# Second batch's tokens ahead of most weights in the load queue; GpSimd forms T3 and T1 of the first pair, VectorE normalises the second batch's rows

## The chip, the cores and the metric

The kernel runs on one NeuronCore of one Trainium2 chip. The metric is device microseconds of one launch. Engines are named as in the profile: PE (TensorE matmuls), PEld (its weight loads), DVE (VectorE), ACT (ScalarE), POOL (GpSimd) and SP, whose queue (SPq) issues every DMA of this kernel.

## The reference

Four batches of 512 tokens by 512 features. Cut to what matters:

```python
def xattn(teacher_logits, ctx, Wq, bq, Wk, bk):           # ctx: 4 x 512 x 256
    query, key = ctx @ Wq.T + bq, ctx @ Wk.T + bk          # 4 x 512 x 128
    attention = softmax(query @ key.T, axis=-1)            # 4 x 512 x 512
    return einsum('bln,bmn->blm', teacher_logits, attention)

def ffn(x, W_up, W_gate, W_down):                          # 512 -> 2048 -> 512
    # each weight: round(w / mean|w|) clipped to -1, 0, 1, times mean|w|
    up, gate = x @ ternary(W_up).T, x @ ternary(W_gate).T
    return (silu(up) * gate) @ ternary(W_down).T

x = x + tanh(g_xattn[0]) * xattn(layernorm(x), ctx, Wq, bq, Wk, bk)
x = x + tanh(g_ffn[0]) * ffn(layernorm(x), W_up, W_gate, W_down)
```

The scale of a ternary weight is the mean of all its absolute values, so no unit of it can be rounded before all of it has been loaded and summed.

## The kernel before, in words

**Two stages.** In the first, the attention stage, PE computes for each batch b queries and keys, the energies, the transposed softmax, and then the mix of tokens with attention. DVE adds the mixed result to the token rows in `x_sb`, takes their statistics and normalises them into `xf`. In the second stage, 16 numbered units n of the feed-forward layer run over pairs of batches: (0, 1) and then (2, 3). It begins with the first `product1(0)`, lines 870 and 872.

**Products of quarters.** Matrix products are done in Winograd's form: seven products of quarter blocks in place of eight, with sums of blocks as operands. The sums of the normalised rows are called T1 to T4; B11, B21 and B22 are plain blocks. `xf_half(b, h)` is one half of the features of batch b's normalised rows. T3 is `xf_half(1,1) - xf_half(1,0)`; T1 is `xf_half(1,0) - xf_half(0,0)` and is written over `xf_half(1,0)`, so it must follow T3; T2 and T4 are made from them later. Each such block is written as a high and a low half of 16 bits (`high_t` on ACT, L1141; `low_t` on DVE, L1545), and SP transposes both by DMA for PE. The mixing of batches 0 and 1 is in the same form: `mix_product(b, j)` (PE, L786) with j in the order 1, 5, 6, 3, 7, 2, 4. Its operands are sums of the transposed tokens, made by `x_sums(b)` (POOL, L573 to L578) from `xT`, and sums of the attention, made by `p_sums_1(b)` and `p_sums_2(b)` (POOL, L582 to L589). Batches 2 and 3 are mixed plainly, by `mix(b, i)` (L763), a tile of 128 tokens at a time.

**Every engine has its order written out by hand**, and waits for the others by semaphores. The orders around the change:

- SP issues the loads one after the other. `load_ug(m, c)` (L400) is 1 MiB of the up (m = 0) or gate (m = 1) weight, `load_x(b)` (L389) 1 MiB of token rows, `load_xt(b, i)` (L397) 256 KiB of transposed tokens, `load_ctx(b)` (L386) 512 KiB of context. `load_ctx(2)` waits for PE to have read the context before it.
- POOL runs `x_sums(1)`, then four short groups of scalar arithmetic for layer norm, in this order: `rstd1_two(1,0)`, `rstd2_two(0,0)`, `rstd1_two(1,1)`, `rstd2_two(0,1)` (L558 to L568), then `p_sums_1(1)` and `p_sums_2(1)`. rstd1 is for the statistics of the token rows as loaded, rstd2 for those after the mix. `x_sums(1)` begins with a wait for all four tiles of batch 1's transposed tokens. Later POOL normalises batch 1's rows (`norm_x1`, L594, four tiles), and then in `rstd2(2, i)` and `rstd1(2, i + 2)` (L600, L601 and L548 to L551) serves batch 2, with three small instructions (L649 to L651) between that make the scales of the weights.
- ACT takes the sums of absolute values with `sum_abs(m, c)` (L1086), the exponentials with `exp_row(b, i)` (L1100), scales the rows with `norm_p` (L1105), copies transposed attention with `copy_at` (L1109), and makes the high halves, T3 and T1 among them.
- DVE adds the mix with `add_mixed(b, j)` (L1505, batches 0 and 1) or `make_x1(b, i)` (L1493, batches 2 and 3), takes the rows' maxima (`row_max`, L1471), the reciprocals of the exponential sums (`row_rsum`, L1475) and the statistics (L1482 to L1519), normalises (`norm_x1`, L1527) batches 0, 2 and 3, and makes T3 and T1 of the first pair (L1636, L1638) behind `norm_x1(2, 0)`.

"Two" in a helper's name means two tiles at once. `hold` is a wait with an empty instruction behind it, so that the engine itself stops.

Of the kernel before, what the change touches and what calls it, by code (L numbers as in the profile page):

```python
# [6 lines left out]
def gated_block_kernel(nc, x, xT, first, ctxT, wqkT, wugT, wdT, x1_dram, out):  # L7
# [19 lines left out]
    NT = ROWS // P  # L27
    NE = wdT.shape[1]
    WCOLS = NE * KD * P
    NABS = 4  # L30
# [15 lines left out]
    with stack:  # L46
# [103 lines left out]
        s_half = sem("s_half")  # L150
        s_ss, s_ts, s_mp, s_xe, s_x2p = (sem(n) for n in ("s_ss", "s_ts", "s_mp", "s_xe", "s_x2p"))
        s_dt, s_ev, s_shift = sem("s_dt"), sem("s_ev"), sem("s_shift")
# [229 lines left out]
        def _(sp):  # L382
# [39 lines left out]
            load_x(1)  # L422
            load_ug(0, 1)
            load_ug(0, 2)
            load_ctx(2)
            load_ug(0, 3)
            load_ug(1, 0)
            for i in range(NT):
                load_xt(1, i)
                if i < 3:  # L430
                    load_ug(1, i + 1)
            load_x(2)
# [87 lines left out]
        def _(pool):  # L520
# [69 lines left out]

            def norm_x1(b, i):
                hold(pool, s_r2, b * NT + i + 1)
                g = b * NT + i
                pool.tensor_scalar(xn_tile(b, i), rows(x_tile(b, i)), mv2[:, g, 0:1], r2[:, g:g + 1],  # L594
                                   ALU.subtract, ALU.mult).then_inc(s_x2p, 1)

            def rstd2(b, i):
# [37 lines left out]
            rstd1(2, 1)  # L635
            for h in range(2):
                rstd2_two(1, h)
                norm_x1(1, 2 * h)
                norm_x1(1, 2 * h + 1)
            for b in range(NS, NB - 1):  # L640
                for i in range(NT):
                    rstd2(b, i)
                    if i + 2 < NT:
# [430 lines left out]
        def _(act):  # L1074
# [86 lines left out]
            for b in range(NB):  # L1161
# [18 lines left out]
                for i in range(NT):  # L1180
# [42 lines left out]
                    if last:  # L1223
                        if i == 0:
                            act.wait_ge(s_t2, 1)
                            high_t(0, "T2", xf_half(0, 0))
                            act.wait_ge(s_x2p, NT)
                            high_t(0, "B22", xf_half(1, 1))
                            round_unit(1)
                        if i == 1:  # L1230
                            sign_unit(1)
                        if i == 2:
                            round_unit(2)
# [81 lines left out]
            def sign_down(c):  # L1315

                act.wait_ge(s_dround, c)
                act.wait_ge(d_spill, 16 * 8)
                act.wait_ge(s_x2n, NG - NT if c > 1 else 2 * NT)
                act.activation(t_d[:, c * ACOLS:(c + 1) * ACOLS], xt_flat[:, :], ACT.Sign, bias=nmagic).then_inc(s_tda, 1)  # L1320
# [10 lines left out]
            for n in range(G1 - 1):  # L1331
# [50 lines left out]
                if n == 5:  # L1382
                    act.wait_ge(s_td, 4)
                    act.wait_ge(s_x2n, NG - NT)
                    high_t(NU, "B11", xf_half(2, 0))
# [82 lines left out]
        def _(dve):  # L1468
# [102 lines left out]
            for b in range(NS):  # L1571
# [28 lines left out]
                if b == 0:  # L1600
                    rows_in(1, 3)
                    norm_x1(0, 0)
                    norm_x1(0, 1)
                else:
                    low_t(0, "B21", xf_half(0, 1))

            for b in range(NS, NB):
                last = b == NB - 1
                for i in range(NT):
# [23 lines left out]
                    if b == 2:  # L1633
                        if i == 0:
                            hold(dve, s_x2p, NT)
                            dve.tensor_tensor(t3_sb, xf_half(1, 1), xf_half(1, 0), ALU.subtract).then_inc(s_t3, 1)  # L1636
                            hold(dve, s_t3, 1)
                            dve.tensor_tensor(xf_half(1, 0), xf_half(1, 0), xf_half(0, 0), ALU.subtract)\  # L1638
                                .then_inc(s_t1, 1)
                        if i == 1:  # L1640
# [102 lines left out]
            for n in range(G1 - 1):  # L1743
# [57 lines left out]
                if n == 4:  # L1801
                    norm_x1(NB - 1, 2)
                    norm_x1(NB - 1, 3)
                    hold(dve, s_x2n, NG - NT)
                    dve.wait_ge(d_tb["T4"], d_tb_done(0, "T4"))
# [153 lines left out]
```

## Time and profile before

| | us |
|---|---|
| median of 3 runs | 412.23 (411.55 to 412.46) |
| the profiled execution, its own time | 412.31 |
| its span, first to last instruction | 410.5 |
| PE busy | 391.2 (95%) |
| DVE busy | 316.2 (77%) |
| ACT busy | 267.3 (65%) |
| POOL busy | 173.6 (42%) |

The profiled execution's own time is 1.8 us longer than its span. Times in the rows are counted from the span's start. The attention stage ends at 109.3 us, where the first `product1` starts; a change in the attention stage is worth what it moves that start, unless a later wait takes it back.

### The profile page before, as it was taken

Reading aid. Unit: us, or ns where it says so; the run is one execution under the profiler, and the core shown is the slowest. Engines: PE = TensorE matmul, PEld = TensorE weight load, DVE = VectorE, ACT = ScalarE, POOL = GpSimd, SP = SyncE. Lnnn points to the kernel's source line nnn. Section 1 sums busy time; section 2 is a strip of 40 time slices with the busy share of each in tenths; the row PEclk is TensorE's granted clock in tenths of the full one; section 3 lists DMA queues with packets and bytes.
Section 4 is the critical chain, followed back from the end, with each engine's and each line's share of the span. In section 5 each row is a group of like instructions: output and inputs, shape, how many; then the busy total and the mean of one; then the engine's idle time right before and its main releaser. Section 6 shows DMA issues by size and latency. Waiting matters only on the chain.

```text
span 410.5 us, 6058 instructions
## 1 busy us (share of the span) xinstructions
PE 391.2 (95%) x1944; PEld 215.5 (52%) x1952; DVE 316.2 (77%) x473; ACT 267.3 (65%) x360; POOL 173.6 (42%) x189
## 2 busy tenths in 40 slices
PE   8999079989999999999999999999999999999997
PEld 6576057544444444444444444444444656656886
DVE  1866268588888998478888886577869998798984
ACT  3887166867987878686898875466277775564400
POOL 0850871965798502240406300535356574461000
PEclk9999669999999999999999999999999999999999
DMA  8999912729960003002002963024230000000014
GB/s 300 414 417 401 405 60 44 173 99 255 215 172 20 0 1 104 0 14 91 0 2 66 192 116 76 15 77 129 102 103 2 2 2 0 2 2 0 2 51 155
DMA packets 43183, 43.91 MB, mean 107 GB/s; under 512 B 30992, under 2 KB 33168, under 8 KB 41104
## 3 DMA queue, kind: packets, MB, share of 16 engines
q1 hardware_dynamic: 43152, 43.53, 34.2%
q8 instruction: 16, 0.26, 0.3%
q14 instruction: 15, 0.12, 0.1%
HBM read 29.89 MB, written 6.29 MB: 88 GB/s over the span
## 4 chain that ended last, share of the span: by engine, by line
PE 76%; DMA 5%; DVE 5%; POOL 5%; issue 5%; ACT 2%; SPq 1%; DVEq 0%; POOLq 0%; ACTq 0%
PE pair L870 22%; PE pair L872 22%; PE pair L944 13%; PE pair L988 11%; DMA xb_lo<-in_xT 5%; PE pair L763 3%; PE pair L786 2%; POOL xf L594 1%; DVE small L1471 1%; DMA xf<-in_first 1%; POOL small L568 1%; PE pair L736 1%; DVE xf L1674 1%; ACT sh L1100 1%; SPq L400 1%
## 5 line engine op out<-in xcount | busy, mean ns | idle before, releaser
L870 PE MATMUL pair<-xb_hi,w_sb 128*128 128x512 f16 x448 | 169.8, 379 | 0.2 <-DVE xf L1669 0.2
L872 PE MATMUL pair<-xb_lo,w_sb 128*128 128x512 f16 x448 | 169.8, 379 | 0.0
L870 PEld LDWEIGHTS pair<-xb_hi,w_sb 128*128 128x128 bf16 x448 | 43.9, 98 | 52.5 <-ACT xf L1297 0.7
L872 PEld LDWEIGHTS pair<-xb_lo,w_sb 128*128 128x128 bf16 x448 | 43.9, 98 | 51.1 <-issue 0.3
L1248 ACT ACTIVATE xf<-xf,small 128x512 f32<-128x512 f32 x48 | 34.5, 720 | 52.4 <-DVE xf L1669 31.6
L944 PE MATMUL pair<-x_sb,sh 128*128 128x512 bf16 x248 | 55.1, 379 | 0.4
L1674 DVE SCALAR_TENSOR_TENSOR xf<-xf,small 128x512 f32<-128x512 f32 x48 | 40.0, 836 | 8.4 <-ACT xf L1248 8.4
L944 PEld LDWEIGHTS pair<-x_sb,sh 128*128 128x128 f16 x256 | 24.8, 98 | 30.7 <-DVE x_sb L1711 0.9
L607 POOL TENSOR_TENSOR w_sb<-w_sb 128x512 bf16<-128x512 bf16 x8 | 9.6, 1196 | 63.1 <-ACT w_sb L1122 63.1
L1679 DVE TENSOR_TENSOR sh<-xf,sh 128x512 f16<-128x512 f32 x36 | 32.1, 899 | 0.7 <-ACT sh L1259 0.7
L1725 DVE SCALAR_TENSOR_TENSOR x_sb<-pair,small,x_sb 128x256 f32<-128x256 f32 (+1 forms) x57 | 25.5, 474 | 5.9 <-PE pair L988 5.4
L1711 DVE SCALAR_TENSOR_TENSOR x_sb<-pair,small,x_sb 128x512 f32<-128x512 f32 x32 | 23.9, 747 | 7.8 <-PE pair L944 7.7
L1259 ACT ACTIVATE sh<-xf 128x512 f16<-128x512 f32 x36 | 22.1, 623 | 10.5 <-DVE xf L1674 9.3
L763 PE MATMUL pair<-sh,xt_sb 128*128 128x512 f32 (+2 forms) x80 | 28.6, 508 | 0.0
L695 POOL TENSOR_TENSOR xf<-xf 128x512 f32<-128x512 f32 x7 | 9.8, 1405 | 44.2 <-DMA xb_lo<-xf 28.2
L1664 DVE TENSOR_TENSOR xf<-pair,xf 128x1024 f32<-128x1024 f32 x16 | 19.5, 1221 | 8.8 <-PE pair L872 8.6
L1659 DVE TENSOR_TENSOR xf<-pair,xf 128x1024 f32<-128x1024 f32 x16 | 19.5, 1221 | 4.1 <-issue 1.6
L1669 DVE TENSOR_TENSOR xf<-pair,xf 128x1024 f32<-128x1024 f32 x16 | 19.5, 1220 | 4.1 <-PE pair L872 3.9
L1285 ACT ACTIVATE xf<-pair 128x1024 f32<-128x1024 f32 x16 | 16.4, 1022 | 8.1 <-PE pair L872 7.6
L1100 ACT ACTIVATE sh<-pair,small 128x512 f32<-128x512 f32 x16 | 10.9, 683 | 15.2 <-DVE small L1471 15.1
L763 PEld LDWEIGHTS pair<-sh,xt_sb 128*128 128x128 f32 x80 | 13.9, 190 | 12.6 <-issue 10.5
L1674 DVE SCALAR_TENSOR_TENSOR c<-c,small,pair 128x512 f32<-128x512 f32 x16 | 11.9, 742 | 10.1 <-ACT c L1248 10.1
(199 smaller groups left out, 731.5 us busy)
## 6 DMA issues: line engine op xcount, KB each, us to landing
w_sb<-in_wugT SPq DMA_DIRECT2D x8, 1024.0 KB, 14.0
x_sb<-in_x SPq DMA_DIRECT2D x4, 1024.0 KB, 12.0
xf<-in_wdT SPq DMA_DIRECT2D x4, 1024.0 KB, 7.0
xt_sb<-in_wdT SPq DMA_DIRECT2D x4, 1024.0 KB, 4.8
xt_sb<-in_xT SPq DMA_DIRECT2D x12, 256.0 KB, 5.7
x_dram<-x_sb SPq DMA_DIRECT2D x8, 256.0 KB, 3.3
out<-x_sb SPq DMA_DIRECT2D x8, 256.0 KB, 2.0
x_sb<-x_dram SPq DMA_DIRECT2D x2, 1024.0 KB, 6.1
```

The source lines that it names most:

```text
L763: last = pe.matmul(ps_x[i % 2][:, lo:hi], xt_tile(b, i)[:, k, :], at[:, k, lo:hi], start=(k == 0), stop=(k == KD - 1))
L870: pe.matmul(dst[:, m * 512:(m + 1) * 512], w[:, o:o + P], hi[:, k], start=start and k == 0, stop=False, skip_group_check=not start)
L872: last = pe.matmul(dst[:, m * 512:(m + 1) * 512], w[:, o:o + P], lo[:, k], start=False, stop=k == 1, skip_group_check=not start)
L944: ins = pe.matmul(dst, h_part(n, c, lo)[:, i * P:(i + 1) * P], t_d[:, e * DM + lo_col:e * DM + hi_col], start=first and n == units[0] and ...
L988: ins = pe.matmul(fin_bank(g, j, t), hidden(u, c, lo, min(t, NT - 1)), cols, start=first and u == units[0] and lo == 0 and not (side and t ...
L1248: act.activation(cb(n, c)[:, 0:512], src, ACT.Silu, scale=su[:, :]).then_inc(s_silu[c], 1)
L1259: act.activation(part(n, c, 0), shaped(n, c, cb(n, c)[:, 0:512]), ACT.Copy).then_inc(s_hi[c], 1)
L1659: dve.tensor_tensor(cb(n, "11"), ps_y[:, :], cb(n, "11"), ALU.add).then_inc(s_c["11"], 1)
L1674: dve.scalar_tensor_tensor(cb(n, c)[:, 0:512], cb(n, c)[:, 0:512], kap[:, :], gate, ALU.mult, ALU.mult).then_inc(s_mul[c], 1)
L1679: dve.tensor_tensor(part(n, c, 1), shaped(n, c, cb(n, c)[:, 0:512]), part(n, c, 0), ALU.subtract)\
L1711: dve.scalar_tensor_tensor(y_tile(b, i), at, c_out[:, :], y_tile(b, i), ALU.mult, ALU.add)\
L1725: dve.scalar_tensor_tensor(fin_rows(g, j, t), fin_bank(g, j, t), c_out[:, :], fin_rows(g, j, t), ALU.mult, ALU.add).then_inc(s_ef, 1)
```

## The change

SP: the four tiles `xT[1, i]` are issued two behind the second MiB of the up weight and two behind the third, ahead of `load_ctx(2)`; before, they stood between the four MiB of the gate weight. POOL: it no longer runs `norm_x1(1, i)`; both `rstd2_two` follow each other, then POOL makes T3, and T1 ahead of `rstd2(2, 1)`. DVE: it runs `norm_x1(1, 0)` and `norm_x1(1, 1)` ahead of the low half of B21 and `norm_x1(1, 2)` and `norm_x1(1, 3)` behind it, and no longer makes T3 and T1. The rows of batch 1 are now counted by `s_x2n`, so waits on it count four more; `s_x2p` is gone. The operations themselves are the same.

```diff
             load_ug(0, 0)
             load_x(1)
             load_ug(0, 1)
+            load_xt(1, 0)
+            load_xt(1, 1)
             load_ug(0, 2)
+            load_xt(1, 2)
+            load_xt(1, 3)
             load_ctx(2)
             load_ug(0, 3)
-            load_ug(1, 0)
-            for i in range(NT):
-                load_xt(1, i)
-                if i < 3:
-                    load_ug(1, i + 1)
+            for c in range(NABS):
+                load_ug(1, c)
             load_x(2)
...
-            for h in range(2):
-                rstd2_two(1, h)
-                norm_x1(1, 2 * h)
-                norm_x1(1, 2 * h + 1)
+            rstd2_two(1, 0)
+            rstd2_two(1, 1)
+            hold(pool, s_x2n, 2 * NT)
+            pool.tensor_tensor(t3_sb, xf_half(1, 1), xf_half(1, 0), ALU.subtract).then_inc(s_t3, 1)
             for b in range(NS, NB - 1):
                 for i in range(NT):
+                    if i == 1:
+                        hold(pool, s_t3, 1)
+                        pool.tensor_tensor(xf_half(1, 0), xf_half(1, 0), xf_half(0, 0), ALU.subtract).then_inc(s_t1, 1)
                     rstd2(b, i)
...
                 else:
+                    norm_x1(1, 0)
+                    norm_x1(1, 1)
                     low_t(0, "B21", xf_half(0, 1))
+                    norm_x1(1, 2)
+                    norm_x1(1, 3)
...
                     if b == 2:
-                        if i == 0:
-                            hold(dve, s_x2p, NT)
-                            dve.tensor_tensor(t3_sb, xf_half(1, 1), xf_half(1, 0), ALU.subtract).then_inc(s_t3, 1)
-                            hold(dve, s_t3, 1)
-                            dve.tensor_tensor(xf_half(1, 0), xf_half(1, 0), xf_half(0, 0), ALU.subtract)\
-                                .then_inc(s_t1, 1)
```

**The load queue.** The difference of SP's order, where the weights `w_sb` and batch 1's transposed tokens (`xb_lo`) are issued:

```order
-L400 DMA w_sb<-in_wugT 128x2048 x2
+L400 DMA w_sb<-in_wugT 128x2048
+L397 DMA xb_lo<-in_xT 128x512 x2
+L400 DMA w_sb<-in_wugT 128x2048
+L397 DMA xb_lo<-in_xT 128x512 x2
 L386 DMA sh<-in_ctxT 128x1024 [waits s_proj]
-L400 DMA w_sb<-in_wugT 128x2048 x2
-L397 DMA xb_lo<-in_xT 128x512
-L400 DMA w_sb<-in_wugT 128x2048
```

The first two issues of tokens now stand ahead of `load_ug(0, 2)`, and all four ahead of the context load that waits on `s_proj`; `load_ug(0, 3)` and the four MiB of the gate weight follow that wait.

**GpSimd between batch 1's second layer norm and batch 2's.** Before:

```order
L594 TENSOR_SCALAR xf<-x_sb,small 128x2x256 [waits s_r2] x2
L600 TENSOR_SCALAR small<-small 128x1 [waits s_ln2]
L601 TENSOR_TENSOR small<-small 128x1 [waits s_pool]
L548 TENSOR_SCALAR small<-small 128x1 [waits s_ln1]
L549 TENSOR_TENSOR small<-small 128x1 [waits s_pool]
L550 TENSOR_TENSOR small<-small 128x1 [waits s_pool]
L551 TENSOR_SCALAR small<-small 128x1 [waits s_pool]
L649 TENSOR_SCALAR small<-small 128x1 [waits s_red]
L650 TENSOR_TENSOR small<-small 128x1 [waits s_cf]
L651 TENSOR_SCALAR small<-small 128x1 [waits s_cf]
```

And now:

```order
L634 TENSOR_TENSOR t_sb<-xf 128x1024 [waits s_x2n]
L595 TENSOR_SCALAR small<-small 128x1 [waits s_ln2]
L596 TENSOR_TENSOR small<-small 128x1 [waits s_pool]
L549 TENSOR_SCALAR small<-small 128x1 [waits s_ln1]
L550 TENSOR_TENSOR small<-small 128x1 [waits s_pool]
L551 TENSOR_TENSOR small<-small 128x1 [waits s_pool]
L552 TENSOR_SCALAR small<-small 128x1 [waits s_pool]
L647 TENSOR_SCALAR small<-small 128x1 [waits s_red]
L648 TENSOR_TENSOR small<-small 128x1 [waits s_cf]
L649 TENSOR_SCALAR small<-small 128x1 [waits s_cf]
L639 TENSOR_TENSOR xf<-xf 128x1024 [waits s_t3]
```

T3 (L634) took the place of the normalising, and T1 (L639) now stands behind it and nine scalar instructions of GpSimd's own, the last three of which make the weights' scales.

**VectorE in the same place.** Before, from the statistics of batch 1's last rows:

```order
L1519 BN_AGGR small<-small 128x2 [waits s_bs] x2
L1545 TENSOR_TENSOR xb_lo<-xf,xb_hi 128x1024 [waits s_th]
L1493 SCALAR_TENSOR_TENSOR x_sb<-pair,small,x_sb 128x512 [waits s_r1,s_xm]
```

And now:

```order
L1517 BN_AGGR small<-small 128x2 [waits s_bs] x2
L1525 TENSOR_SCALAR xf<-x_sb,small 128x2x256 [waits s_r2] x2
L1543 TENSOR_TENSOR xb_lo<-xf,xb_hi 128x1024 [waits s_th]
L1525 TENSOR_SCALAR xf<-x_sb,small 128x2x256 [waits s_r2] x2
L1491 SCALAR_TENSOR_TENSOR x_sb<-pair,small,x_sb 128x512 [waits s_r1,s_xm]
```

Four instructions of normalising (L1525) stand ahead of the first `make_x1`.

## Rows read from the trace of the kernel before

**Rows 1.** Single DMA issues, in order; the last number: us from issue to landing.
```profile
w_sb<-in_wugT SPq DMA_DIRECT2D x1, 1024.0 KB, 15.4
...
xb_lo<-in_xT SPq DMA_DIRECT2D x1, 256.0 KB, 18.7
```

**Rows 2.** Timeline of SP: start us, us, engine, line, what.
```profile
6.51 1.64 SPq L400 DMA_DIRECT2D w_sb<-in_wugT  x2
```

**Rows 3.** Timeline of GpSimd, 25 to 54 us.
```profile
25.15 1.27 POOL L589 TENSOR_TENSOR xf<-sh,xf 128x512 f32<-128x512 f32 x1
40.39 1.27 POOL L573 TENSOR_TENSOR xb_hi<-xb_lo 128x512 f32<-128x512 f32 x1 [13.97 <-DMA xb_lo<-in_xT]
...
49.18 0.19 POOL L558 TENSOR_SCALAR small<-small 128x2 f32<-128x2 f32 x1
...
52.51 1.26 POOL L582 TENSOR_TENSOR xf<-sh 128x512 f32<-128x512 f32 x1
```

**Rows 4.** Timeline of TensorE, 20 to 60 us.
```profile
20.61 3.62 PE L786 MATMUL pair<-xf 128*128 128x256 f32 x16
...
40.11 1.88 PE L736 MATMUL pair<-sh 128*128 128x512 f32 x4
53.91 6.06 PE L786 MATMUL pair<-xf,xb_hi 128*128 128x256 f32 x16 [11.93 <-POOL xf L582]
```

**Rows 5.** Timeline of VectorE, 38 to 50 us.
```profile
38.24 0.18 DVE L1488 BATCH_NORM_AGGREGATE small<-small 128x2 f32<-128x6 f32 x1
49.20 1.00 DVE L1527 TENSOR_SCALAR xf<-x_sb,small 128x512 f32<-128x512 f32 x2 [10.78 <-POOL small L568]
```

**Rows 6.** Stretch: us; busy PE, PEld, DVE, ACT, POOL; PEclk, DMA share, GB/s.
```profile
45.00:46.00 1.00, 0.00 (x0) 0.00 (x0) 0.00 (x0) 0.00 (x0) 0.88 (x2) 0.53 0.98 410
```

**Rows 7.** Timeline of ScalarE, 42 to 89 us.
```profile
42.86 0.19 ACT L1086 ACTIVATION_READ_ACCUMULATOR xb_lo<-w_sb 128x1 f32 x1
51.68 0.69 ACT L1100 ACTIVATE sh<-pair,small 128x512 f32<-128x512 f32 x1 [8.63 <-DVE small L1471]
...
60.50 0.19 ACT L1086 ACTIVATION_READ_ACCUMULATOR xb_lo<-w_sb 128x1 f32 x1
...
85.96 1.05 ACT L1141 ACTIVATE xb_hi<-xf 128x1024 f16<-128x1024 f32 x1
87.96 0.69 ACT L1100 ACTIVATE sh<-pair,small 128x512 f32<-128x512 f32 x1 [0.95 <-DVE small L1471]
```

**Rows 8.** Timeline of VectorE, 77 to 81 us.
```profile
77.47 0.75 DVE L1493 SCALAR_TENSOR_TENSOR x_sb<-pair,small,x_sb 128x512 f32<-128x512 f32 x1 [3.15 <-PE pair L763]
...
80.12 0.17 DVE L1519 BATCH_NORM_AGGREGATE small<-small 128x2 f32<-128x6 f32 x1
```

**Rows 9.** Timeline of GpSimd, 81 to 101 us.
```profile
81.80 0.19 POOL L600 TENSOR_SCALAR small<-small 128x1 f32<-128x1 f32 x1
...
82.80 0.19 POOL L548 TENSOR_SCALAR small<-small 128x1 f32<-128x1 f32 x1
...
85.91 0.19 POOL L649 TENSOR_SCALAR small<-small 128x1 f32<-128x1 f32 x1
...
86.81 0.19 POOL L651 TENSOR_SCALAR small<-small 128x1 f32<-128x1 f32 x1
...
98.59 0.19 POOL L548 TENSOR_SCALAR small<-small 128x1 f32<-128x1 f32 x1
...
100.50 0.26 POOL L551 TENSOR_SCALAR small<-small 128x1 f32<-128x1 f32 x1 [0.18 <-POOL small L550]
```

**Rows 10.** Groups by form, of GpSimd, then of VectorE: busy us, mean ns.
```profile
L677 POOL TENSOR_TENSOR xf<-xf 128x1024 f32<-128x1024 f32 x1 | 2.9, 2869 | 0.0
L679 POOL TENSOR_TENSOR xf<-xf 128x1024 f32<-128x1024 f32 x1 | 2.6, 2624 | 0.1
...
L1638 DVE TENSOR_TENSOR xf<-xf 128x1024 f32<-128x1024 f32 x1 | 1.2, 1226 | 0.1
```

**Rows 11.** Timeline of TensorE, at 89 us.
```profile
89.81 0.66 PE L747 MATMUL pair<-early,sh 128*128 128x128 f32 x4 [1.20 <-ACT sh L1105]
```

More of the change, by code:

```diff
@@ L150, in gated_block_kernel @@
         s_half = sem("s_half")
-        s_ss, s_ts, s_mp, s_xe, s_x2p = (sem(n) for n in ("s_ss", "s_ts", "s_mp", "s_xe", "s_x2p"))
+        s_ss, s_ts, s_mp, s_xe = (sem(n) for n in ("s_ss", "s_ts", "s_mp", "s_xe"))
         s_dt, s_ev, s_shift = sem("s_dt"), sem("s_ev"), sem("s_shift")
@@ L589, in p_sums_2 @@
                 pool.tensor_tensor(p_sum(b, 3), p_quarter(b, 1, 0), p_sum(b, 1), ALU.subtract).then_inc(s_ts, 1)
[L591 to L595, printed above, removed]
             def rstd2(b, i):
@@ L1226, in _ @@
                             high_t(0, "T2", xf_half(0, 0))
-                            act.wait_ge(s_x2p, NT)
+                            act.wait_ge(s_x2n, 2 * NT)
                             high_t(0, "B22", xf_half(1, 1))
@@ L1318, in sign_down @@
                 act.wait_ge(d_spill, 16 * 8)
-                act.wait_ge(s_x2n, NG - NT if c > 1 else 2 * NT)
+                act.wait_ge(s_x2n, NG if c > 1 else 3 * NT)
                 act.activation(t_d[:, c * ACOLS:(c + 1) * ACOLS], xt_flat[:, :], ACT.Sign, bias=nmagic).then_inc(s_tda, 1)
@@ L1383, in _ @@
                     act.wait_ge(s_td, 4)
-                    act.wait_ge(s_x2n, NG - NT)
+                    act.wait_ge(s_x2n, NG)
                     high_t(NU, "B11", xf_half(2, 0))
@@ L1803, in _ @@
                     norm_x1(NB - 1, 3)
-                    hold(dve, s_x2n, NG - NT)
+                    hold(dve, s_x2n, NG)
                     dve.wait_ge(d_tb["T4"], d_tb_done(0, "T4"))
```

## The prediction

> **What bounds the kernel now.** I read the table of busy times first: PE is busy for 95% of the span, so time can come only from the places where PE waits, or where it works slowly. The list of who waited for whom puts one wait far ahead of the others: PE stood still for 11.9 us before the sixteen matmuls of `mix_product(1, 5)` and `(1, 6)`, and the timeline names GpSimd's L582, the first of `p_sums_1(1)`, as what ended it [rows 4]. So the next view is GpSimd's timeline. It was free at 26.4, stood for 13.97 us until the last tile of batch 1's transposed tokens had landed, and then worked without a pause from 40.39 to 52.51, where L582 starts [rows 3]. That tile was issued at 21.5 and took 18.7 us to land [rows 1], behind the four MiB of the gate weight, which nobody needs that soon. The second thing to see is the clock: TensorE's granted clock is 0.53 in the microsecond from 45 to 46 [rows 6], the mean of its two levels, 2.4 GHz and 1.2 GHz, with the fall at once behind 45, about 3 us after PE's last matmul ended. The matmuls that follow the wait took 6.06 us where sixteen of the same shape took 3.62 at full clock [rows 4]. After 109 us there is almost no waiting; a shift of that point shifts the end.
>
> **The load queue.** Transfers land in the order of their issue: the third MiB of the up weight was issued at 7.7 and landed 15.4 us later, at 23.1 [rows 1, 2], at some 2.5 us a MiB. In the new order 1 MiB of tokens is issued around it, ahead of the context load and its wait on PE, so the last token tile lands one MiB later than 23.1, at about 25.7. GpSimd is free at 26.4 [rows 3]. So GpSimd starts `x_sums(1)` at 26.5 instead of 40.39. The first MiB of the up weight keeps its place, the third is late by two tiles (1.3 us, at 24.4, still before ScalarE turns to it), and the gate weight's last MiB lands near 39.8, as before, well before its sum.
>
> **GpSimd's chain.** Its start comes 13.9 us earlier, but not all of it arrives. `x_sums(1)` and the first two scalar groups are done by about 36.3, and then `rstd1_two(1,1)` needs the statistics of batch 1's last rows, which VectorE has at 38.42 (38.24 and 0.18) [rows 5]. This is the next thing that is late. From the start of that group to L582 GpSimd took 52.51 - 49.18 = 3.33 us [rows 3], beside the same normalising by VectorE; so L582 starts at 38.55 + 3.33 = 41.9 instead of 52.51: **10.6 us earlier**. The slack of this step is 2.2 us: if tokens land that much later, nothing changes.
>
> **The clock.** PE ends its own work at 41.9 (40.11 and 1.88, less the overlap of ends) and now waits until 43.3, 1.4 us instead of 11.93. A wait of that length lies inside the 3 us in which the clock had not yet fallen. The sixteen matmuls then take 3.6 and not 6.06 us: **2.4 us**, if nothing else holds PE there; the next in line is ScalarE. Its sum of the gate weight's second MiB ends at 43.05 [rows 7], so the exponentials of batch 2 start there and not at 51.68, 8.6 us earlier; from there to the end of the last sum, which PE needs for the weights' scale, it took 9.0 us (51.68 to 60.69), of which about 1 us was VectorE's waiting behind GpSimd's sums, and shrinks. That gives 51.1 to 52.1. PE, done with the sixteen at 46.9, has 4.7 us of matmuls before the scale's (sixteen more of 256 columns at 3.5 us, two of 512 and a transpose) and comes to it at 51.6. So between 0 and 0.5 us of the 2.4 may be lost; I take 2.4, since no row shows that microsecond whole, and keep the end at 1.2 for losses in this closely meshed piece. PE then starts `mix(2, 0)` 10.6 + 2.4 = **13.0 us** earlier.
>
> **VectorE and GpSimd change places.** From here times are in before's clock, that is 13.0 us late. VectorE is about 0.9 us less early than PE, since it starts from ScalarE's exponentials. It had stood 3.15 us before its first `make_x1` at 77.47 [rows 8]; the four normalising instructions are two pairs of 1.00 us [rows 5], 2.0 us in all, and fit in the 2.25 left. They cost nothing; without that cover they would cost up to 2.0. T3 on GpSimd can start at 77.4. GpSimd's two prices for this shape are 2.87 and 2.62 [rows 10]; I take 2.75. T3 ends at 80.2, before `rstd2(2, 0)` gets its statistics at 80.29 [rows 8]. So T3 is hidden, with nothing to spare, and comes to ScalarE earlier than before.
>
> T1 is not. GpSimd's order in front of it: `rstd2(2, 0)` 1.0 us (81.80 to 82.80) from 80.4, to 81.5; `rstd1(2, 2)`, which took 3.1 us (82.80 to 85.91) beside VectorE's T3 and T1, and 2.2 (98.59 to 100.76) beside one normalising [rows 9]. That second case is what stands there now: 83.8. The scales' three instructions, 1.1 us [rows 9]: 84.9. T1: 87.7. ScalarE turns it into a high half for 1.05 us, and only then comes `exp_row(3, 2)`, which started at 87.96 [rows 7]: it now starts at 88.9. **1.0 us is given back**, at PE's wait of 1.20 us at 89.81 [rows 11], which becomes 2.2. The bounds: with `rstd1` at 1.7 (2.2 less the normalising) and T1 at 2.62, 0.3 us; with 3.1 and 2.87, 1.9 us. VectorE has lost two instructions of 1.23 us [rows 10], but the time goes nowhere: it waits in `row_rsum(3, 2)` for the same exponential. Everything behind (`make_x1(2, 2)`, `exp_row(3, 3)`, the mix of batch 3, the transposes, the first `product1`) follows that exponential as it did.
>
> A rule speaks against this part. The Trainium skill, GPSIMD Engine Reference, section Engine selection, gives elementwise work on a tile to VectorE, and GpSimd as about twice as slow for two inputs (its measured ratio is 1.96). By that ratio, an estimate from the page, T1 would take 1.96 x 1.23 = 2.4 us and the sum would be 0.35 us lower; this trace's 2.62 to 2.87 against 1.23 is 2.1 to 2.3 times, and the rows decide.
>
> **The sum.** -10.6 - 2.4 + 1.0 = -12.0 us against the profiled execution's 412.31 gives **400.3 us** (span 398.5). The median of the runs, 412.23, is the same within 0.1.
>
> **The rivals.**
> (a) *T1 comes in time.* ScalarE gets it before its turn, if GpSimd's scalar groups run as short as undisturbed. Then the 1.0 us stays, and VectorE's 2.45 freed microseconds shorten PE's wait of 1.20: 399.3 to 398.6. For it: the bound of 0.3. Against: nine scalar instructions stand ahead of T1.
> (b) *ScalarE or VectorE holds PE between 43 and 60*, so that the clock's part is half or nothing, or T1 costs its upper bound: 412.3 - 10.6 - 1.2 + 1.9 = 402.4, at worst 403.6. For it: 0.5 us of slack or less at two places.
> (c) *The tokens don't come earlier.* If the queue shared its bandwidth among all that is outstanding instead of serving in order, the last tile would land with the last weights, GpSimd would start at 40.4 as before, and T1's 1.0 us would remain: 413.3, **slower**. It decides from the point where GpSimd's L582 comes less than 1 us earlier, that is where `x_sums(1)` starts later than 39.4. Against it: a MiB issued 14 us before the last tile landed 17 us before it [rows 1, 2], behind nothing but its own predecessors.
> (d) *A part of the chain is missing from this account*, such as statistics or the context of batch 2, so that half of the 13 us arrives: 406 us. Against it: every landing that was looked at is 1 us or more ahead of its use.
>
> **How the numbers follow.** Forecast 0.60; (a) 0.15; (b) 0.17; (d) 0.06; (c) 0.02. The forecast is 400.3; from (a) the range goes down to 398.7, from (b) up to 402.8. About 0.2% of 412 us, 0.8 us, is what a measurement can tell from no change. Faster by more than that: all but (c): 0.97; within it 0.01; slower 0.02.
>
> **What would show it.** In the new profile: GpSimd's L574 starts at 26.5, its L583 at 41.9; PE's wait before the sixteen matmuls is 1.4 us; the granted clock is 1.00 everywhere from 20 to 60 us; PE starts the mix of batch 2 at 60.8; GpSimd's T1 ends at about 74.7 (87.7 in before's clock), and ScalarE stands idle for it for over 2 us, where its high half of T1 began at 85.96 before [rows 7]; PE's wait for the attention of batch 3 is 2.2 us; the first `product1` starts at 97.3. The prediction is wrong if PE stands still for over 3 us anywhere in that stretch, or if T1's wait is absent.

## The result and the profile after

The changed kernel takes **400.47 us** (median of 4 runs, 399.24 to 400.93), the kernel before 412.35 us (4 runs, 411.55 to 412.93): a ratio of **0.9709**, 95% interval 0.9679 to 0.9738. The forecast was 400.3 us in a range of 398.7 to 402.8. The profiled execution took 400.03 us with a span of 398.2 us. Two single runs among the experiments lie far off all others (2362.87 us with the exchange alone, 691.3 us with T1 early) and are left out of the medians below.

The page of the changed kernel: busy times, then in 40 slices GpSimd and the clock, and the head of the chain that ended last.

```profile
PE 389.4 (98%) x1944; PEld 214.4 (54%) x1952; DVE 316.0 (79%) x475; ACT 267.0 (67%) x360; POOL 169.5 (43%) x187
...
POOL 0685824757995005131428001525359556271000
PEclk9999999999999999999999999999999999999999
...
PE 84%; DVE 5%; issue 3%; ACT 3%; POOL 3%; DMA 1%; DVEq 0%; POOLq 0%; ACTq 0%
```

PE has the same matmuls and is now busy for 98% of a shorter span, and the clock is at 2.4 GHz in every slice. The rest of the reading follows the steps of the prediction, from the queue to the first `product1`.

**SP**, the issues of tokens and weights (start us, us, engine, line, what):

```profile
7.61 1.23 SPq L397 DMA_DIRECT2D xb_lo<-in_xT  x2
8.88 0.60 SPq L400 DMA_DIRECT2D w_sb<-in_wugT  x1
9.53 2.52 SPq L397 DMA_DIRECT2D xb_lo<-in_xT  x2
18.54 0.33 SPq L386 DMA_DIRECT2D sh<-in_ctxT  x1
18.91 2.33 SPq L400 DMA_DIRECT2D w_sb<-in_wugT  x5
```

All four token tiles are issued by 12.1 us; before, the last one was issued at 21.5. They landed 13.6 to 15.5 us after their issue, the last one (issued at 11.5, 14.2 us) at 25.7, which is the forecast's own figure.

**GpSimd**, from the end of batch 0's sums to `p_sums_1(1)`, the same columns and then the idle time before the instruction with its releaser:

```profile
26.34 1.27 POOL L590 TENSOR_TENSOR xf<-sh,xf 128x512 f32<-128x512 f32 x1
27.57 1.26 POOL L574 TENSOR_TENSOR xb_hi<-xb_lo 128x512 f32<-128x512 f32 x1
...
39.27 0.36 POOL L559 TENSOR_SCALAR small<-small 128x2 f32<-128x2 f32 x1 [2.29 <-DVE small L1486]
...
42.80 1.26 POOL L583 TENSOR_TENSOR xf<-sh 128x512 f32<-128x512 f32 x1
```

The 13.97 us of [rows 3] are gone: L574 follows straight on its predecessor. What is late next is the statistics of batch 1's last rows, for 2.29 us, as foretold. L583 starts at 42.80 instead of 52.51.

**TensorE**, 40 to 100 us:

```profile
40.78 1.88 PE L734 MATMUL pair<-sh 128*128 128x512 f32 x4
44.21 3.69 PE L784 MATMUL pair<-xf,xb_hi 128*128 128x256 f32 x16 [1.54 <-POOL xf L583]
...
61.72 3.63 PE L761 MATMUL pair<-sh,xt_sb 128*128 128x384 f32 x16
...
77.69 0.65 PE L745 MATMUL pair<-early,sh 128*128 128x128 f32 x4 [1.15 <-ACT sh L1103]
...
82.70 0.66 PE L745 MATMUL pair<-early,sh 128*128 128x128 f32 x4 [0.92 <-ACT sh L1103]
...
97.19 0.38 PE L868 MATMUL pair<-xb_hi,w_sb 128*128 128x512 f16 x1
```

Against [rows 4]: the wait of 11.93 us is one of 1.54, and the sixteen matmuls behind it take 3.69 us and not 6.06. Against [rows 11]: the wait of 1.20 us, which was to grow to 2.2, is 1.15. The first `product1` comes at 97.19; before, it came at 109.33.

**ScalarE**, around the high half of T1:

```profile
74.89 1.06 ACT L1139 ACTIVATE xb_hi<-xf 128x1024 f16<-128x1024 f32 x1 [2.98 <-POOL xf L639]
75.86 0.67 ACT L1098 ACTIVATE sh<-pair,small 128x512 f32<-128x512 f32 x1
```

ScalarE does stand for T1, 2.98 us. The exponential behind it (`exp_row(3, 2)`) starts at 75.86, 12.10 us earlier than the 87.96 of [rows 7], which is the same 12.1 us by which PE's mix of batch 2 came earlier (61.72 against 73.80): nothing was given back between them.

**GpSimd** in the same place:

```profile
64.22 2.37 POOL L634 TENSOR_TENSOR t_sb<-xf 128x1024 f32<-128x1024 f32 x1 [1.64 <-DVE xf L1525]
...
69.62 0.38 POOL L549 TENSOR_SCALAR small<-small 128x1 f32<-128x1 f32 x1 [0.35 <-DVE small L1486]
...
71.22 0.27 POOL L552 TENSOR_SCALAR small<-small 128x1 f32<-128x1 f32 x1 [0.18 <-POOL small L551]
...
72.50 2.35 POOL L639 TENSOR_TENSOR xf<-xf 128x1024 f32<-128x1024 f32 x1
```

T3 and T1 took 2.37 and 2.35 us, less than either price in [rows 10], and `rstd1(2, 2)` 1.87 us (69.62 to 71.49).

### The profile page after: what moved, and what is told of

The parts are those of the page before. It is cut to its first block, busy times and chain, and to the rows that moved or that the text cites. A ratio compares the mean times of both kernels' runs of the same rounds, so it can differ in the third digit from the quotient of the medians.

```text
span 398.2 us, 6058 instructions
## 1 busy us (share of the span) xinstructions
PE 389.4 (98%) x1944; PEld 214.4 (54%) x1952; DVE 316.0 (79%) x475; ACT 267.0 (67%) x360; POOL 169.5 (43%) x187
## 4 chain that ended last, share of the span: by engine, by line
PE 84%; DVE 5%; issue 3%; ACT 3%; POOL 3%; DMA 1%; DVEq 0%; POOLq 0%; ACTq 0%
PE pair L868 22%; PE pair L870 22%; PE pair L942 14%; PE pair L986 11%; PE pair L784 5%; PE pair L761 4%; PE pair L734 2%; PE pair L720 1%; PE pair L745 1%; ACT sh L1098 1%; DVE small L1469 1%; DMA xf<-in_first 1%; PE pair L799 1%; DVE xf L1670 1%; POOL xf L639 1%
## 5 line engine op out<-in xcount | busy, mean ns | idle before, releaser
L1721 DVE SCALAR_TENSOR_TENSOR x_sb<-pair,small,x_sb 128x256 f32<-128x256 f32 (+1 forms) x57 | 25.5, 472 | 5.9 <-PE pair L986 5.4
L761 PEld LDWEIGHTS pair<-sh,xt_sb 128*128 128x128 f32 x80 | 13.9, 190 | 12.6 <-issue 10.5
L1114 ACT ACTIVATE w_sb<-w_sb,small 128x1024 f32<-128x1024 f32 x16 | 18.9, 1227 | 0.0
```

The lines of the kernel that those rows point to most:

```text
L761: last = pe.matmul(ps_x[i % 2][:, lo:hi], xt_tile(b, i)[:, k, :], at[:, k, lo:hi], start=(k == 0), stop=(k == KD - 1))
L1721: dve.scalar_tensor_tensor(fin_rows(g, j, t), fin_bank(g, j, t), c_out[:, :], fin_rows(g, j, t), ALU.mult, ALU.add).then_inc(s_ef, 1)
```

## The experiments

Two theories stood at the start. **A**, the prediction's: all of the gain is the load order, 10.6 us of wait and 2.4 us of clock, and T1's place on GpSimd costs something. **B**: the exchange of work between VectorE and GpSimd has a part in the gain. Later a third question came up, why the start of the trace did not match. The kernel before was timed beside each group of runs: 412.6 us beside the first four kernels, 412.9 beside the next four, 412.25 beside the last four.

### 1. The loads alone, and the exchange alone

The first kernel is before with the new load order and nothing else; the second is the changed kernel with the old order:

```diff
             load_ug(0, 1)
-            load_xt(1, 0)
-            load_xt(1, 1)
             load_ug(0, 2)
-            load_xt(1, 2)
-            load_xt(1, 3)
             load_ctx(2)
             load_ug(0, 3)
-            for c in range(NABS):
-                load_ug(1, c)
+            load_ug(1, 0)
+            for i in range(NT):
+                load_xt(1, i)
+                if i < 3:
+                    load_ug(1, i + 1)
```

> Kernel before with the new load order alone. Theory (the load order carries all of the gain, the exchange of work between VectorE and GpSimd nets to nothing): 400.1 to 400.7 us, and TensorE's wait before the sixteen matmuls is about 1.5 us. Rival 1 (the exchange itself carries part, since VectorE lost 2.45 us of two-input work): 401.5 us or more. Rival 2 (the exchange cost 1.0 us, as the prediction had it): 399.4 us.

> Kernel before with the exchange of work alone, loads in the old order. Theory: within 0.5 us of the kernel before, 411.9 to 412.9 us. Rival 1: faster, 411 us or less. Rival 2 (the exchange costs 1.0 us): 413.3 us.

Measured: the loads alone 400.6 us (400.48 to 400.89), ratio 0.9706 (0.9686 to 0.9726); the exchange alone 412.62 us (11 runs, 411.66 to 413.96), ratio 1.0002 (0.9988 to 1.0016). TensorE with the loads alone:

```profile
44.71 3.69 PE L787 MATMUL pair<-xf,xb_hi 128*128 128x256 f32 x16 [1.55 <-POOL xf L583]
```

TensorE with the exchange alone:

```profile
54.87 5.26 PE L783 MATMUL pair<-xf,xb_hi 128*128 128x256 f32 x16 [11.37 <-POOL xf L582]
```

ScalarE with the exchange alone:

```profile
87.12 1.06 ACT L1138 ACTIVATE xb_hi<-xf 128x1024 f16<-128x1024 f32 x1 [3.07 <-POOL xf L638]
```

The load order carries the whole gain, and the exchange is worth nothing in either order of the loads. Theory B falls, and so does the 1.0 us that theory A charged: ScalarE stands for T1 (2.98 and 3.07 us), but PE's wait is the same with T1 on VectorE (1.22 us there) and on GpSimd (1.15).

### 2. T1 earlier, T1 later

If T1's place costs nothing, is it because it just comes in time, or because something else is as late? First T1 was put right behind T3:

```diff
             pool.tensor_tensor(t3_sb, xf_half(1, 1), xf_half(1, 0), ALU.subtract).then_inc(s_t3, 1)
+            hold(pool, s_t3, 1)
+            pool.tensor_tensor(xf_half(1, 0), xf_half(1, 0), xf_half(0, 0), ALU.subtract).then_inc(s_t1, 1)
             for b in range(NS, NB - 1):
                 for i in range(NT):
-                    if i == 1:
-                        hold(pool, s_t3, 1)
-                        pool.tensor_tensor(xf_half(1, 0), xf_half(1, 0), xf_half(0, 0), ALU.subtract).then_inc(s_t1, 1)
                     rstd2(b, i)
```

> Changed kernel with T1 made right behind T3 on GpSimd, ahead of rstd2(2, 0). Theory (in the changed kernel the exponential of batch 3's third row waits for T1 alone, by way of ScalarE's high half): ScalarE gets T1 at about 69 and not at 74.9 us, exp_row(3, 2) starts at about 73 and not at 75.9, TensorE's waits of 1.15 and 0.92 us for the attention of batch 3 shrink or vanish, and the time falls by 1.0 to 2.1 us, to 398.4 to 399.5. Rival (that exponential is bound by VectorE's row maximum or another wait): no change, 400.5.

Measured: **398.05 us** (median of 4 runs, 397.76 to 398.69), ratio 0.9645 (0.9625 to 0.9666), 2.4 us below the changed kernel, a little more than the 1.0 to 2.1 expected. GpSimd of this kernel:

```profile
67.05 2.35 POOL L636 TENSOR_TENSOR xf<-xf 128x1024 f32<-128x1024 f32 x1
```

Its ScalarE, behind that:

```profile
71.95 1.05 ACT L1138 ACTIVATE xb_hi<-xf 128x1024 f16<-128x1024 f32 x1
...
73.15 0.69 ACT L1097 ACTIVATE sh<-pair,small 128x512 f32<-128x512 f32 x1 [0.15 <-DVE small L1468]
```

And its TensorE, at the first `product1`:

```profile
95.00 0.38 PE L867 MATMUL pair<-xb_hi,w_sb 128*128 128x512 f16 x1
```

ScalarE no longer stands for T1. T1 is ready at 69.4, and ScalarE turns to it at 71.95, when its own earlier work is done (I had expected 69). PE has no wait at all left between 44.5 and 90 us: both the 1.15 and the 0.92 us are gone, which are most of the 2.4. So T1 was late in both kernels, by about the same. Before, it held up VectorE, for which the exponential waited 0.95 us [rows 7]; now it comes late itself, behind nine scalar instructions of GpSimd, and ScalarE's high half of T1 stands ahead of the exponential. That the second of the two waits went because VectorE is rid of T3 and T1 is what I take from it; T1 early on VectorE was not tried.

Then T1 was made later, by repeating the scales' power four times ahead of it (the same value each time):

```diff
-                        coef(pool.tensor_tensor(kap[:, :], kap0[:, :], mone[:, :], ALU.pow))
+                        for _ in range(5):
+                            coef(pool.tensor_tensor(kap[:, :], kap0[:, :], mone[:, :], ALU.pow))
```

> Changed kernel in which GpSimd repeats one scalar instruction four times among the scales of the weights, ahead of T1, so that T1 comes about 2.5 us later. Theory (T1 has no slack in the changed kernel: exp_row(3, 2) starts as soon as ScalarE has its high half): the time rises by the whole 2.3 to 2.6 us, to about 402.9. Rival (T1 is hidden and the exponential is bound by something else): it rises by under 1.5 us.

Measured: 403.32 us (6 runs, 402.9 to 406.63), ratio 0.9781: 2.85 us above the changed kernel, a little more than the 2.3 to 2.6 expected. TensorE in its profiled execution, which was the slowest of the six:

```profile
82.41 1.12 PE L746 MATMUL pair<-early,sh 128*128 128x128 f32 x4 [3.65 <-ACT sh L1104]
83.31 5.98 PE L762 MATMUL pair<-sh,xt_sb 128*128 128x512 f32 x8
```

and the stretches around it (us; busy PE, PEld, DVE, ACT, POOL; granted clock as a share of 2.4 GHz, DMA share, GB/s):

```profile
80.00:82.00 2.00, 0.00 (x0) 0.00 (x0) 0.57 (x3) 1.70 (x4) 0.67 (x2) 0.82 0.00 0
82.00:84.00 2.00, 1.59 (x5) 1.25 (x6) 2.00 (x3) 2.00 (x2) 1.71 (x3) 0.50 0.00 0
```

PE's wait grew from 1.15 to 3.65 us and ScalarE's for T1 from 2.98 to 5.65, so lateness of T1 reaches PE nearly one for one. And in this execution the clock fell to 1.2 GHz (0.50) within that wait, so that the eight matmuls behind it took 5.98 us (eight of this shape took 3.60 in the changed kernel). This execution was late from its start as well: the four matmuls that section 5 counts from began at 22.30, later than in any other profile. The other five runs have no profile, but each run's mean granted clock is on record: 0.992 in the profiled one, 0.995 in four of the others and 1.000 in one. So the clock fell in those four too; they took 402.90 to 403.40 us, the one without a fall 402.91, so there the fall cost half a microsecond at most.

### 3. The clock by itself

Before, with eleven extra matmuls on PE inside its long wait (their result is used by nothing):

```diff
                     energy(b + 1, 1)
+                    if b == 1:
+                        for _ in range(11):
+                            pe.matmul(ps_q, ones[:, :], k_sb, start=True, stop=True)
                     mix_product(b, 5)
```

> Kernel before with eleven matmuls of 512 columns, whose results are not used, put into TensorE's wait of 11.9 us, so that it idles for 2 to 3 us only. Theory (2.4 us of the gain are the clock's): the granted clock stays at 1.00, the sixteen matmuls take 3.7 and not 6.06 us, and the time falls by 1.8 to 2.4 us, to 409.9 to 410.6. Rival (ScalarE and VectorE hold TensorE there anyway): the matmuls are quicker but the start of the mix of batch 2 moves by under 1 us, 411.4 or more.

Measured: 411.2 us (12 runs, 410.02 to 412.46), ratio 0.9965 (0.9949 to 0.9981), 1.4 us below before. TensorE (the trace shows each of these fp32 matmuls as two):

```profile
42.92 9.61 PE L831 MATMUL pair<-sh,early 128*128 128x512 f32 x22
54.58 3.69 PE L786 MATMUL pair<-xf,xb_hi 128*128 128x256 f32 x16 [2.06 <-POOL xf L582]
```

The sixteen matmuls have the same releaser as before and take 3.69 us. The mix of batch 2 starts at 72.10, 17.52 us behind them; before it was 19.89 (53.91 to 73.80). So in the two profiles the clock is worth the 2.37 us that the prediction had, and nothing else held PE there. The medians differ by 1.4 us, below the 1.8 to 2.4 that I expected. The mean granted clock of each run shows why: eight of the twelve runs have 0.999 or 1.000 and a median of 410.8 us, which is 1.8 below; the other four have 0.995 or 0.996 and took 411.8 to 412.5 us. There the clock fell in spite of the extra matmuls; where, no profile shows. Section 5 adds that before itself does not always lose 2.4.

### 4. How much slack the tokens have, and what is late next

The tokens behind two more transfers, the context of batch 2 (whose issue waits on PE) and the last MiB of the up weight:

```diff
             load_ug(0, 1)
-            load_xt(1, 0)
-            load_xt(1, 1)
             load_ug(0, 2)
-            load_xt(1, 2)
-            load_xt(1, 3)
             load_ctx(2)
             load_ug(0, 3)
+            for i in range(NT):
+                load_xt(1, i)
```

> Changed kernel with batch 1's token tiles issued behind the context load and the fourth MiB of the up weight, ahead of the gate weight: they land at about 31 and not 26 us, x_sums(1) starts about 3.9 us later. Theory (the next late thing is batch 1's statistics, so the first 3 us of a later landing cost nothing): GpSimd's first p_sum comes 0.7 to 1.2 us later and the time rises by as much, to 401.2 to 401.7. Rival (every microsecond of landing counts): 404.4.

Measured: 400.45 us (5 runs, 400.08 to 400.7), ratio 0.9702 (0.9688 to 0.9715): no change. GpSimd:

```profile
30.75 1.27 POOL L572 TENSOR_TENSOR xb_hi<-xb_lo 128x512 f32<-128x512 f32 x1 [3.45 <-DMA xb_lo<-in_xT]
...
39.70 0.19 POOL L557 TENSOR_SCALAR small<-small 128x2 f32<-128x2 f32 x1 [0.18 <-DVE small L1484]
```

`x_sums(1)` starts 3.2 us later than in the changed kernel, and the wait for statistics shrinks from 2.29 to 0.18 us. I had expected 0.7 to 1.2 us of loss; PE waits no longer than before (1.25 us). The slack of 2.2 us that the prediction named is real, and it is nearer to 3: in the changed kernel GpSimd had waited 2.29 us for these statistics and 0.76 us for others just ahead of them.

The statistics earlier, by VectorE's rows of batch 1 ahead of its next mixed tile:

```diff
                 rows_out(b, 0)
+                if b == 0:
+                    rows_in(1, 3)
                 add_mixed(b, 4)
                 rows_out(b, 1)
                 if b == 0:
-                    rows_in(1, 3)
                     norm_x1(0, 0)
```

> Changed kernel in which VectorE takes the statistics of batch 1's last tile ahead of add_mixed(0, 4) and not behind the rows' second statistics. Theory (these statistics are what the remaining wait of 1.54 us comes from): GpSimd's first p_sum comes about 2 us earlier, TensorE's wait before the sixteen matmuls vanishes, a wait of about 0.4 us for ScalarE's scaled rows of batch 2 takes its place, and the time falls by 1.0 to 1.5 us, to 399.0 to 399.5. Rival (VectorE's and ScalarE's own chain takes all of it): 400.2 or more.

Measured: 399.95 us (4 runs, 399.58 to 400.37), ratio 0.9689 (0.9675 to 0.9703), 0.5 us below the changed kernel. That is less than the 1.0 to 1.5 expected, and its interval overlaps the changed kernel's (0.9679 to 0.9738), so by the times alone it is not told apart. TensorE:

```profile
43.34 3.62 PE L784 MATMUL pair<-xf,xb_hi 128*128 128x256 f32 x16
47.90 0.66 PE L745 MATMUL pair<-early,sh 128*128 128x128 f32 x4 [0.94 <-ACT sh L1103]
```

The wait of 1.54 us is gone, so the statistics were its cause, but a wait of 0.94 us for ScalarE, where 0.4 was expected, stands five microseconds behind it and takes back most of the gain: ScalarE waits 1.22 us for VectorE's reciprocal, which comes behind a pair of its normalising instructions, stretched to 2.87 us beside GpSimd's sums. VectorE there:

```profile
44.15 2.87 DVE L1525 TENSOR_SCALAR xf<-x_sb,small 128x512 f32<-128x512 f32 x2
```


Both edits together (T1 behind T3, statistics early):

> T1 right behind T3 and the early statistics together. Theory: the two gains stand at different places and add up, 2.1 and about 1.1 us: 396.9 to 397.5 us. Rival (they share a bound): no better than T1 early alone, 398.2.

Measured: 397.93 us (4 runs, 397.29 to 399.0), ratio 0.9642 (0.9625 to 0.9659), the lowest median of all, though only 0.1 us below T1 early alone, less than such runs can tell apart. I had expected 396.9 to 397.5.

### 5. The start

One thing in the first comparison did not fit. PE's four matmuls of line L734 began at 20.07 us in the changed kernel and at 18.90 before (L736), with nothing of the change ahead of them on PE. (They are the first two energies of batch 1, each shown as two; the expectation below calls them the second query projection.) So both kernels were profiled twice more, unaltered:

> The changed kernel, unaltered, profiled again. In the profiled execution of the changed kernel PE's four matmuls of the second query projection (L734) began at 20.07 us, where before's began at 18.90 (L736); I put that down to the start-up (when the second half of the first load lands), which varies from execution to execution, and to nothing in the change. Theory: from those four matmuls to the first product1 this kernel always takes 97.19 - 20.07 = 77.1 us, since no transfer is waited for in between; so whatever the start gives, first product1 = start of the four + 77.1 within 0.6, and span = that + 301.0. Rival: the end does not follow the start, because slack or a transfer absorbs it; then the first product1 stays within 0.3 of 97.2 whatever the start.

> The changed kernel, unaltered, a third profile: the same two expectations as for the second. Over the executions of this kernel the start of the four matmuls should scatter over 18.9 to 21 us, and the span with it, one for one.

> The kernel before, unaltered, profiled again. Here a transfer stands in the chain (GpSimd waits for the last token tile, then PE for GpSimd). Theory: the start of PE's four matmuls (L736; 18.90 before) scatters as in the changed kernel, but the end follows it less than half, since the tile's landing decides: with a start 1 us later, x_sums(1) at 40.4 to 40.9 and the first product1 at 109.3 to 109.9. Rival: the end follows it one for one here too (110.3).

> The kernel before, unaltered, a third profile: the same two expectations as for the second. A start of the four matmuls above 18.9 with a span within 0.5 us of 410.5 would show that the profiled execution on which the prediction was built happened to start early and that this did not matter for it, while it matters for the changed kernel.

Measured: 400.58 and 399.84 us for the changed kernel, 412.54 and 412.21 for before. The times in the profiles, all starts in us (for the four matmuls L734 or L736, for GpSimd's first `x_sums(1)` L574 or L573):

| execution | four matmuls | `x_sums(1)` | sixteen matmuls, us each time | first `product1` | from the four to it | span |
|---|---|---|---|---|---|---|
| changed, first | 20.07 | 27.57 | 44.21, 3.69 | 97.19 | 77.12 | 398.2 |
| changed, second | 20.66 | 28.18 | 44.80, 3.69 | 97.80 | 77.14 | 398.8 |
| changed, third | 19.82 | 27.33 | 43.96, 3.69 | 96.95 | 77.13 | 398.1 |
| before, first | 18.90 | 40.39 | 53.91, 6.06 | 109.33 | 90.43 | 410.5 |
| before, second | 21.15 | 41.18 | 54.73, 5.40 | 109.49 | 88.34 | 410.7 |
| before, third | 20.22 | 41.04 | 54.59, 5.25 | 109.19 | 88.97 | 410.4 |

Where the time is lost can be seen at PE's first real work. TensorE before, first profile:

```profile
3.99 2.04 PE L801 MATMUL pair<-xf 128*128 128x256 f32 x8
```

The same in the second profile of before:

```profile
4.07 3.42 PE L801 MATMUL pair<-xf 128*128 128x256 f32 x8 [0.16 <-DMA xf<-in_first]
```

I had put this down to the landing of `in_first`, the load that these matmuls read. The rows don't bear that out: its two halves landed 3.2 and 3.6 us after their issue in the first profile and 3.3 and 3.8 in the second, which is 0.1 to 0.2 us, while the next matmuls start 1.47 us later (7.33 against 5.86). What differs is the speed. The weight loads of these eight matmuls, from 3.8 to 7.3 us (busy us, mean ns of one | idle before), first profile and then second:

```profile
L801 PEld LDWEIGHTS pair<-xf 128*128 128x128 f32 x8 | 1.3, 195 | 0.5 <-DMA xf<-in_first 0.4
...
L801 PEld LDWEIGHTS pair<-xf 128*128 128x128 f32 x8 | 2.3, 327 | 0.8 <-DMA xf<-in_first 0.5
```

The same kind of weight load in the first profile from 54.8 to 57.4 us, where the granted clock is 1.2 GHz (0.50):

```profile
L786 PEld LDWEIGHTS pair<-xf,xb_hi 128*128 128x128 f32 x7 | 2.4, 337 | 0.6
```

So in the second profile PE still ran at 1.2 GHz here. The trace's record of the granted clock agrees: its first entry, 2.4 GHz, stands at 4.09 us in the first profile of before, at 7.00 in the second and 6.55 in the third, and at 5.36, 6.27 and 5.04 in the three of the changed kernel. (A view of a stretch ahead of that entry prints 1.00, since nothing is recorded there.) The execution whose clock rose first has the earliest four matmuls, 18.90, and the one whose clock rose last the latest, 21.15; the rest of those 2.25 us comes in waits for VectorE before 17.3 us. What sets the moment of the rise, no run shows.

In the changed kernel the lateness of the start arrives at the end one for one: from the four matmuls to the first `product1` it is 77.12 to 77.14 us in all three. Before, 2.25 us of it (18.90 to 21.15) moved the first `product1` by 0.16. GpSimd's wait for the tiles took up most of it (`x_sums(1)` 0.79 later), and the clock nearly all that was left: the sixteen matmuls began 0.82 us later and took 0.66 less, since TensorE was back at 2.4 GHz sooner behind the restart. The stretch of before's first profile from 58 to 59 us (the granted clock is the 0.65):

```profile
58.00:59.00 1.00, 1.00 (x5) 0.81 (x4) 1.00 (x3) 1.00 (x3) 0.00 (x0) 0.65 0.00 0
```

And of its second profile:

```profile
58.00:59.00 1.00, 1.00 (x6) 0.87 (x5) 0.55 (x2) 1.00 (x1) 0.63 (x1) 0.90 0.00 0
```

This bears on section 3 too: the matmuls at half speed cost 2.4 us in the first profile of before (mean granted clock 0.983), and 1.6 to 1.7 in the others (5.25 and 5.40 against 3.69; 0.988). Of the 23 runs of before beside the first four kernels twelve have 0.983 and eleven 0.988, with medians of 412.7 and 412.4 us.

With the start taken out, the other kernels line up much as their medians do. From the four matmuls to the first `product1`: 77.21 with the loads alone, 75.34 with T1 early, 76.50 with statistics early, 74.34 with both, 77.54 with the tokens later. Against 77.12 that is +0.1, -1.8, -0.6, -2.8 and +0.4 us; the medians said +0.1, -2.4, -0.5, -2.5 and 0.0. T1 early and the tokens later carry in their profiles a wait of PE for ScalarE at 25.5 us (0.51 and 0.50) that the changed kernel's three don't have. Counted from the four matmuls behind it (L734 in the changed kernel, at 40.78 us) the five are +0.1, -2.5, -0.6, -2.8 and -0.3.

## Why the prediction was right, point by point

- **The load queue** was right. `x_sums(1)` at 27.57 was forecast at 26.5; the last tile was there at 25.7, so GpSimd and no longer the tile was what `x_sums(1)` waited for; GpSimd was itself 1.2 us later than in [rows 3], with the late start of section 5.
- **GpSimd's chain.** The next late thing was the statistics. L583 was forecast at 41.9 and came at 42.80, 9.7 us earlier than before instead of 10.6. In this trace's own clock the step held: PE's wait was forecast as 1.4 us and was 1.54.
- **The clock.** 1.00 throughout, sixteen matmuls in 3.69 us, forecast 3.6. ScalarE's last sum ended at 50.98, against the 51.1 to 52.1 worked out, and PE lost nothing of the 2.4 us: from the sixteen to the mix of batch 2 it took 17.51 us, as in section 3 with the clock up (17.52), and 19.89 before. That confirms the value taken and not rival (b).
- **Mix of batch 2**: forecast at 60.8, measured 61.72, which is 12.1 us earlier and not 13.0. **This step failed, by 0.9 us.** 0.7 of it is the start (batch 1's last statistics were ready at 39.10 and not at 38.42), and 0.2 is GpSimd's scalar group behind them, which took 3.53 us to L583 and not 3.33. The sum was made "against the profiled execution's 412.31": that execution of before had the earliest start of six (18.90; the others 19.82 to 21.15), and before hid that start, so that its time was still the median. The changed kernel does not hide it. From the four matmuls to the mix it is 41.65 us (20.07 to 61.72), where the forecast's times give 41.9 (18.90 to 60.8).
- **VectorE's normalising and T3** cost nothing, as forecast. T3 took 2.37 us.
- **"1.0 us is given back"** was the second failed term: it was 0, below its own lower bound of 0.3. T1 was priced at 2.75 us by the nearest rows and took 2.35; `rstd1(2, 2)` at 2.2 and took 1.87; T1 thus ended, on the mix's clock, 0.8 us sooner than worked out (74.85 is 13.13 us behind 61.72; the working had 13.9), and the exponential followed its end by 1.0 us, where the working had 1.2. ScalarE's standing for T1 was there as foretold, only without a cost to PE. T1's 2.35 us are 1.9 times the 1.23 of VectorE in [rows 10]. The Trainium skill (GPSIMD Engine Reference, Elementwise — side-by-side cycle accounting) gives a ratio of 1.96 for a two-input operation of 2048 fp32 elements, so here the page was nearer than my rows. Those come from a stage where VectorE works with two inputs beside GpSimd, which I take for the reason; no run isolates it.
- The two errors, +0.9 and -1.0 us, have nothing to do with each other and cancel: that 400.3 was hit to 0.2 is luck. Each alone would have stayed in the range.
- **Rivals.** (a) T1 in time: right in its cost, wrong in its reason, since ScalarE did wait for T1. Its other half, VectorE's freed time shortening PE's wait, came only with T1 early, and then PE's next wait (0.92 us) went too: 398.05 us, below the 398.6 of this rival and the 398.7 of the range, which differ by 0.1 without a reason given. (c) tokens not earlier: refuted at the first row of GpSimd. (d) a missing part: nothing of 6 us, but a small one, the start.

## What to carry to other kernels

A wait for a transfer hides much of what is late ahead of it: here 2.25 us of start became 0.16. With the wait gone, the scatter of the start reached the end whole, so a sum against one profiled execution should be made from a point behind the start, or against several profiles. Where an operation moves to a less busy engine, its place in that engine's order can be worth more than its duration: T1 behind nine scalar instructions saved nothing, in front of them 2.4 us. Matmuls or weight loads that take longer than their like should be checked for the clock before a load is blamed. And order a load queue by who needs what first: here 12 us hung on one MiB of tokens behind four of weights.

## What the runs showed of the hardware

- GpSimd's two-input instruction of 128x1024 in fp32 took 2.35 to 2.37 us in the attention stage of the changed kernel, and 2.62 to 2.87 us later in the same program [rows 10].
- VectorE's pair of normalising instructions takes 1.00 us with at most short scalar instructions of GpSimd beside it [rows 5] and 2.15 to 2.87 us beside GpSimd's sums. In the changed kernel:

```profile
39.03 1.00 DVE L1525 TENSOR_SCALAR xf<-x_sb,small 128x512 f32<-128x512 f32 x2
...
43.31 2.45 DVE L1525 TENSOR_SCALAR xf<-x_sb,small 128x512 f32<-128x512 f32 x2
```

  One by one, the two slow ones end at 44.34 and 45.76, each 0.3 us behind the end of one of GpSimd's sums (44.06 and 45.47). The Trainium skill (SBUF — State Buffer, SBUF: two separate sides) has GpSimd share a pair of ports with those VectorE instructions that run in a 2-port mode or have two inputs in SBUF: whichever starts first holds the pair for its whole instruction, and the other is blocked. The rows agree with it; no run here shows the ports themselves, or in which mode VectorE ran.
- TensorE's granted clock stayed at 2.4 GHz over waits of 1.15 to 2.06 us in the profiled executions, and fell in waits of 3.65 and 10.99 to 11.93 us. In four of the twelve runs of section 3's kernel, which waits 2.06 us in its profile, the mean clock shows a fall too (0.995 and 0.996).
- At the start TensorE ran at 1.2 GHz until 4.09 to 7.00 us in the six executions of section 5 (9.60 in the profile with T1 late): the same weight load took 327 ns before that and 190 behind it.
- The start of one and the same program (before) varied by 2.25 us between executions whose total time differed by 0.2.
